# Softmax attention inside a six-stage decoder kernel: projection sums turned later, copies and statistics dealt anew, an output product moved by two steps

## The reference

```python
def _L1_attn_ref(x, wq, wk, wv, wo):            # "attention 1"
    q = jnp.einsum('bsd,hkd->bhsk', x, wq.reshape(H, dk, D))   # H 16 heads, dk 16
    k = jnp.einsum('bsd,hkd->bhsk', x, wk.reshape(H, dk, D))
    v = jnp.einsum('bsd,hkd->bhsk', x, wv.reshape(H, dk, D))
    q, k = _apply_rope(q, sin, cos), _apply_rope(k, sin, cos)
    scores = jnp.einsum('bhqk,bhsk->bhqs', q, k) / jnp.sqrt(dk)
    scores = jnp.where(causal, -jnp.inf, scores)
    attn = jax.nn.softmax(scores, axis=-1)
    out = jnp.einsum('bhqs,bhsv->bqhv', attn, v).reshape(B, S, H * dk)
    return jnp.einsum('bsf,df->bsd', out, wo)

def _L1_xattn_ref(hidden_q, kv_c, ...):         # "cross"
    q_big = _apply_rope(einsum(hidden_q @ Wq.T, w_kc_q), ...)  # 16 heads, 192 wide
    scores = einsum(q_big @ W_qr, kv_r @ W_kr)
    ctx_c  = einsum(softmax(scores), kv_r)
    return einsum(ctx_c, w_kc_kv) @ Wo.T

x = x + _L0_attn_ref(_layernorm(x), ...)
x = x + _L0_xattn_ref(ctx_512, _layernorm(x), ...)
x = x + _L0_ffn_ref(_layernorm(x), ...)
x = x + _L1_attn_ref(_layernorm(x), ...)
x = x + _L1_xattn_ref(_layernorm(x), ctx_512, ...)
x = x + _L1_ffn_ref(_layernorm(x), ...)
```

## Time and profile before

| | before |
|---|---|
| median of three runs | 888.65 us (886.97 to 888.88) |
| the profiled execution's own time | 887.54 us |
| its span | 885.8 us |
| TensorE busy | 857.7 us, 97% of the span |
| VectorE, ScalarE, GpSimd busy | 632.3, 435.7, 99.7 us |
| chain that ended last, by engine | PE 81%, DVE 10%, ACT 3%, issue 3% |
| mean granted TensorE clock | 0.992 of full |

### The profile page before, as it was taken

One profiled execution on the slowest core, in us unless ns is written; L12 is line 12 of the kernel. 1 busy time (PEld: TensorE's weight loads), 2 busy tenths in 40 slices (PEclk: granted clock), 3 DMA queues, 4 the chain that ended last, 5 costly groups with the idle time before them and its releaser, 6 DMA issues.

```text
span 885.8 us, 14144 instructions
## 1 busy us (share of the span) xinstructions
PE 857.7 (97%) x5249; PEld 663.9 (75%) x5249; DVE 632.3 (71%) x1396; ACT 435.7 (49%) x1082; POOL 99.7 (11%) x82
## 2 busy tenths in 40 slices
PE   8998999999999989989989999999999999999998
PEld 5675778888888776767766777777776788888886
DVE  4679757666665768876878978889876666666665
ACT  8554544434443469883343535445456443344342
POOL 4001000000000043000322323132300000000000
PEclk9999999999999999999999999999999999999999
DMA  6003111111100140012300000000220111111001
GB/s 197 1 4 125 37 54 42 49 53 53 36 1 1 69 186 2 2 51 103 117 0 1 1 1 1 1 2 0 66 79 1 54 45 45 53 53 36 18 0 48
DMA packets 12586, 37.42 MB, mean 42 GB/s; under 512 B 2080, under 2 KB 4400, under 8 KB 11760
## 3 DMA queue, kind: packets, MB, share of 16 engines
q1 hardware_dynamic: 12496, 36.65, 12.5%
q0 software_dynamic: 32, 0.01, 0.0%
HBM read 35.60 MB, written 1.05 MB: 41 GB/s over the span
## 4 chain that ended last, share of the span: by engine, by line
PE 81%; DVE 10%; ACT 3%; issue 3%; POOL 1%; DMA 1%; SPq 0%; DVEq 0%; POOLq 0%; ACTq 0%
PE ps L1533 75%; PE ps L2189 3%; PE ps L1710 2%; DVE Q L639 2%; POOL outer_rot L1526 1%; DMA X<-in_x 1%; DVE P L625 1%; DVE stats L542 1%; DVE xn L550 1%; ACT probs_q L1412 1%; PE ps L1677 1%; DVE probs_q L995 0%; DVE rope_buf L929 0%; DVE P L658 0%; DVE wlo L916 0%
## 5 line engine op out<-in xcount | busy, mean ns | idle before, releaser
L1320 ACT ACTIVATE h_hi<-weighted_h 128x512 fp32r<-128x512 f32 x100 | 63.2, 632 | 148.2 <-DVE weighted_h L791 146.0
L801 DVE TENSOR_TENSOR h_lo<-weighted_h,h_hi 128x512 fp32r<-128x512 f32 x100 | 69.2, 692 | 66.7 <-ACT h_hi L1320 66.6
L1533 PE MATMUL ps<-xT_first,whi 128*128 128x512 f32 x376 | 109.6, 392 | 0.0
L1533 PE MATMUL ps<-xT_second,whi 128*128 128x512 f32 x376 | 108.5, 391 | 0.0
L828 DVE TENSOR_TENSOR shared_gate<-silu_g,row_shares 128x512 f32<-128x512 f32 x88 | 60.8, 691 | 60.5 <-ACT silu_g L1315 60.4
L1315 ACT ACTIVATE silu_g<-ps 128x512 f32<-128x512 f32 x100 | 59.3, 595 | 71.5 <-PE ps L1533 71.3
L1412 ACT ACTIVATE probs_q<-ps,neg_max 128x256 f32<-128x256 f32 x128 | 58.6, 484 | 48.6 <-DVE neg_max L985 48.6
L1533 PEld LDWEIGHTS ps<-xT_first,whi 128*128 128x128 f32 x376 | 70.0, 188 | 15.9 <-issue 1.5
L1533 PEld LDWEIGHTS ps<-xT_second,whi 128*128 128x128 f32 x376 | 70.1, 188 | 15.1 <-issue 0.7
L1533 PE MATMUL ps<-h_hi,wlo 128*128 128x512 f32 x200 | 77.9, 390 | 0.0
L1533 PE MATMUL ps<-h_hi,whi 128*128 128x512 f32 x188 | 74.0, 394 | 0.4 <-DVE h_lo L801 0.3
(11 more groups left out here) (220 smaller groups left out, 1649.2 us busy)
## 6 DMA issues: line engine op xcount, KB each, us to landing
raw<-in_ffn SPq DMA_DIRECT2D x50, 384.0 KB, 3.0
wx<-in_wx SPq DMA_DIRECT2D x4, 2112.0 KB, 8.5
cx<-in_cx SPq DMA_DIRECT2D x1, 1536.0 KB, 6.5
X<-in_x SPq DMA_DIRECT2D x4, 256.0 KB, 6.9
kvc<-in_kvc SPq DMA_DIRECT2D x1, 1024.0 KB, 14.2
out<-X SPq DMA_DIRECT2D x4, 256.0 KB, 2.2
wqkv<-in_wqkv SPq DMA_DIRECT2D x1, 768.0 KB, 8.2
wqkv<-in_wqkv SPq DMA_DIRECT2D x1, 512.0 KB, 6.8
```

The lines of the kernel that those rows point to most:

```text
L801: v.tensor_tensor(h_lo[:, u % 2, :], weighted_h[:, u % 2, :], h_hi[:, u % 2, :].bitcast(F32), ALU.subtract).then_inc(act_lo[l], 1)
L1320: a.activation(h_hi[:, u % 2, :], weighted_h[:, u % 2, :], ACT.Copy).then_inc(act_hi[l], 1)
L1533: return pe.matmul(o, l, r, start=start, stop=stop, skip_group_check=True)
```

## The change

Five things are written in another order or given to another engine. No arithmetic is added or removed.

1. Ahead of the loop the sums of batch b - 2, not b - 1, are turned in batch b (TensorE and ScalarE), so `turned(0)` comes behind the projections of batch 2, and `turned(1)` behind batch 3's values. VectorE's `tokens_rest1` comes one batch earlier.
2. Bank 3's copy in steps 1, 4 and 7 goes from VectorE to ScalarE (`both_banks_by_vector`); VectorE keeps those of steps 10, 13, 16, 19 and 22.
3. `output(1, b - 1)` comes in the sixth step of a batch, behind its transposes, and not in the fourth: steps 17 and 23 in place of 15 and 21, for batches 0 and 1.
4. The addition and the statistics that belong to these outputs come later: for batch 0 the addition at the head of step 18 and the statistics in step 19 (both in step 16 before), for batch 1 behind the loop (both in step 22 before).
5. In cross's unit 0 `operand_rest(1)` comes ahead of a `rope` and not behind it.

```diff
+        def both_banks_by_vector(n):
+            return n % 3 == 1 and n >= 10
...
             def copy_transposed(n):          # VectorE
                 copy_first_half(n)
-                if n % 3 == 1:
+                if both_banks_by_vector(n):
...
             def attention1():                # VectorE
                 for b in range(NB - 1):
-                    if b >= 1:
-                        tokens_rest1(b + 1)
+                    if b < NB - 2:
+                        tokens_rest1(b + 2)
                     for st in range(2):
                         project1(b, st)
...
                 for n in range(STEPS):
                     turn, k = divmod(n, 3)
                     b = turn // 2 - 1
+                    if b >= 2 and (turn % 2, k) == (0, 0):
+                        add_out(1, b - 2)
                     row_max(n)
...
-                    if b >= 1 and (turn % 2, k) == (1, 1):
-                        add_out(1, b - 1)
-                        norm_statistics(4, b - 1)
+                    if b >= 2 and (turn % 2, k) == (0, 1):
+                        norm_statistics(4, b - 2)
                 copy_transposed(STEPS - 2)
+                add_out(1, NB - 3)
                 copy_transposed(STEPS - 1)
+                norm_statistics(4, NB - 3)
                 reciprocals(NB - 1)
...
             def cross():                     # VectorE
...
                     if w >= 1:
                         copy_transposed(w - 1)
+                    if w == 0:
+                        operand_rest(1)
                     if more:
                         rope(ahead + 2)
-                    if w == 0:
-                        operand_rest(1)
                     normalise_probs(w, 0)
...
             def attention1():                # ScalarE
...
-                    if 1 <= b < NB - 1:
-                        turned(b - 1)
+                    if b >= 2:
+                        turned(b - 2)
                 for n in range(STEPS):
                     turn, k = divmod(n, 3)
                     b = turn // 2 - 1
-                    if n >= 2 and k != 0:
+                    if n >= 2 and not both_banks_by_vector(n - 2):
                         copy_transposed(n - 2)
...
             def attention1():                # TensorE
...
-                    if 1 <= b < NB - 1:
-                        turned(b - 1)
+                    if b >= 2:
+                        turned(b - 2)
...
                     if b >= 0 and (turn % 2, k) == (1, 0):
                         mixed_probabilities(b, 1)
-                        if b >= 1:
-                            output(1, b - 1)
                     if b >= 0 and (turn % 2, k) == (1, 1):
                         mixed_probabilities(b, 2)
+                    if b >= 1 and (turn % 2, k) == (1, 2):
+                        output(1, b - 1)
```

## The result

The changed kernel takes 879.3 us, the median of four executions (878.3, 879.1, 880.7 and 879.5), where the kernel before took 888.2 in the same comparison: the ratio is 0.990, with a 95% interval from 0.988 to 0.992. Forecast were 880.4 us and a range of 877.0 to 884.6. The profiled execution took 878.27 us, its span is 876.5 us and its mean granted clock 0.995; before these were 887.54, 885.8 and 0.992. The two spans differ by 9.3 us.

A forecast was written before the change was run, and what follows sets the result against it. TensorE, busy 97% of the span, was taken as the bound, so only its waits or half-clock stretches count. Gains of 3.5 + 0 + 4.1 + 0.6 = 8.2 us from 887.54 give 879.3, plus 1.1 for the median: 880.4 us, range 877.0 to 884.6.

The forecast's parts named there:

- Part 1: Ahead of the loop: TensorE's waits for GpSimd go, step 0's scores start at 318.4, gain 3.5 us (1.9 to 4.1).
- the late item that the text had named: Ahead of the loop: `project1(2)` waits for `turned(0)` until 315.7 and ends at 318.4, when TensorE is ready.
- Part 2: Attention loop, steps 1, 4 and 7: three copies to ScalarE give 0; 1.5 us lost to 1.6 won at the ends.
- the forecast's own signs of being wrong: TensorE waiting for ScalarE in steps 3 to 9, step 0 waiting for VectorE well behind 318.4, or a new half-clock stretch.
- ScalarE becomes the bound of steps 2 to 9: Rival, loop: new copies wait with exponentials queued behind; gain only 5.2 to 6.7 us, 882.5 us; chance 0.08.
- Part 3: Steps 15 to 18 and loop's end: output product, additions and statistics later gain 4.1 us, 0.9 included (1.7 to 4.5).
- Part 4: Cross: operand's rest moves into VectorE's idle time; gain 0.6 us, 1.98 at most, or a loss of 1.5.
- The loss that the text priced: Cross: the gap of about 2 us behind the latent queries takes the clock down, a loss of 1.5 us.
- The sum: Whole kernel: 3.5 + 0 + 4.1 + 0.6 = 8.2 us gained, to a median of 880.4 us; chance 0.56.
- the falls of the clock come back elsewhere: Rival: two falls of 1.5 us land in remaining gaps (step 7, cross); gain 5.2 us, 883.4 us; chance 0.12.

The follow-up runs named there:

- e3: Kernel before with only the second-bank copies of steps 1, 4 and 7 moved from VectorE to ScalarE: 887.2 against 887.1 us, ratio 1.0002.
- e4: Kernel before with only the rest of cross's second operand put ahead of the rope: 887.5 against 887.1 us, ratio 1.0002.
- e1: Kernel before with only the turned sums one batch later and the rests of the tokens one batch earlier: 883.4 against 887.1 us, ratio 0.9955.
- e5: Changed kernel with the output product back in a batch's fourth step, additions and statistics left late: 881.9 against 887.6 us for the kernel before, ratio 0.9945.
- e8: Changed kernel with the first two maxima of cross's unit 1 ahead of unit 0's second normalisation: 879.0 against 887.6 us before, ratio 0.9918.
- e10: Changed kernel with step 7's scores multiplied twice into the same place, filling TensorE's wait: 879.2 against 887.6 us for the kernel before, ratio 0.9912.
- e11: Changed kernel with VectorE again copying the second bank of steps 1, 4 and 7: 878.2 against 887.5 us for the kernel before, ratio 0.9902.

## Why the prediction was right

**Part 1, 3.5 forecast, 3.66 in the profile.** The mechanism was right piece by piece: step 0's scores were due 12.1 us behind batch 1's projections and came after 11.97, and after 11.95 to 11.99 in all ten profiles of the new order. `project1(2)` waited for `turned(0)` as forecast, ran from 314.89 to 317.61, and was the late item that the text had named: forecast level with TensorE, it ended 0.23 us after TensorE's last turned sums (317.61 against 317.38), and TensorE waited 0.38 (the row names ScalarE, the semaphores VectorE). What the forecast had not said is that only 2.2 us of it are there in every execution: e3 and e4 have the old order without a fall and take 14.14 and 14.19 us, 2.2 more than the new. The rest, about 1.5, is the price of a fall which the profile of before happened to have. At equal clock e1 gives 3.0 (0.4), more than 2.2, probably since the one slope takes out too little for these falls.

**Part 2, forecast 0.** This step failed in its size. The text named the place, "in step 8 the quarter product waits for ScalarE's copy of the queries, which comes some 0.8 later, exactly when TensorE gets there", but TensorE gets there 0.5 us before the old copy and 1.5 before the new, as soon as the clock stays up; I had read its arrival off a profile in which it was at half clock. The part costs 0.8 us by the stage where the clock stays up (25.9 against 25.1), 1.0 (0.3) by e3's times at equal clock, and nothing in the profiled execution, where the fall hides it. TensorE's wait for a copy of ScalarE in steps 3 to 9 is one of the forecast's own signs of being wrong; it is absent from the change's profile and stands with 1.51 us in those of e5, e8 and e10. e11, which takes the part back, shows no gain beyond the error (878.2 against 879.3). The rival "ScalarE becomes the bound of steps 2 to 9" had the right engine and, with 1.5 to 3 us, too high a price (its 882.5 is also 0.2 under the middle of its own gains of 5.2 to 6.7 us).

**Part 3, 4.1 forecast, 4.4 in the profile.** At steps 8 to 19 0.93 against the 0.9 forecast. At the end 3.48 against 3.2: the mixed product starts 4.41 us earlier than at the end of the loop before (0.93 and 3.48), which is 396.6 where the text had 396.9, with the wait of 0.44 for VectorE's copy that it had named and the clock at 1.00. Of the 3.5 us 1.0 is again a fall (19.8 us with it, 18.8 without, e3); 2.5 are there always.

**Part 4, 0.6 forecast, 0.58 in the profile.** Right to the mechanism, the wait of 1.98 replaced by one of 1.93. The loss that the text priced, a clock taken down by the new wait, occurs in two of nine profiles and costs 0.9 us by the stage (25.5 against 24.6), not the whole gap. At these odds it takes 0.2 of the 0.6 in the mean. e4's own time shows nothing of the gain; seven of its twelve executions have a mean clock of 0.990 or less, and where it fell in them is not known.

**The sum** of 8.2 met a measured 8.8 (9.3 between the spans, 0.5 of it from code ahead of the change). Of the 8.8 us only 5.4 are waits that go in every execution, by the stages of profiles without a fall: 2.2 ahead of the loop, -0.8 in steps 0 to 8, 0.9 from there to step 19, 2.5 over the loop's end, 0.6 in cross. The other 3.4 are the price of three falls in this profile of before (ahead of the loop 1.5, step 7 0.9, the loop's end 1.0). The forecast took them from the same profile, so its sum fits the profiled pair. For the mean it is in part luck: with the falls of before at the odds of the table (2 of 4, 6 of 10, 3 of 4) and that in cross, the same stages give about 7.2 us, an estimate, where the means differ by 7.9 against the 52 executions and by 8.7 against the four timed beside the change. The rival "the falls of the clock come back elsewhere" was right in what it said of the clock and in part wrong in its price: a fall that comes back in step 7 costs nothing, one in cross 0.9 and not 1.5.

The Trainium skill (TensorE: Matmul & The Clock Gate, Part 1) says that the window of activity is free-running; by that rule the same wait can have either outcome. The trace agrees as far as it goes: the ten profiles with the wait of 1.48 us show six falls and four without. No run shows that a shift in time alone moves a fall.

## What to carry to other kernels

Split a gain read from one profile into waits and half clock: the waits are there in every execution, a fall behind a given wait only in some, so look at the same stretch in several profiles before its price goes into a sum. When an engine's arrival at a wait is read from a stretch at half clock, work it out at full clock as well, since a wait may stand hidden behind the fall, as ScalarE's 1.5 us did here. Filling a gap that lies in the way of a serial chain (the output product between the last scores and their transposes) paid more here than relieving the engine that was waited for, 2.3 against 1.1 us by e5's stages. And moving work off one engine is not free for the other: behind three copies more in ScalarE's list a fourth, which TensorE waits for, came a microsecond later, and it was the order within that list that gave 1.6 us back.

## What the runs showed of the hardware

A wait of the same 1.48 us at the same instruction took the granted clock down in six of ten profiles and left it at 1.00 in four. Where it fell to 1.2 GHz, 1.7 us of clock time were lost, in two profiles 3.4, and never anything between. Behind a wait of 1.51 to 1.79 us in step 8 it fell in none of five. As long as TensorE had work, no fall was seen behind waits that were all under 1.3 us in any of the fourteen profiles. A single fall cost between nothing and 1.7 us of time: 1.5 and 1.7 ahead of the loop in the old order (15.63 and 15.83 against 14.17 us), 1.0 in step 7 with part 2 absent (26.06 against 25.11) and nothing there in the change, 1.0 at the loop's end (19.8 against 18.8), 0.9 in cross.
